# First group norm's scale behind the projection instead of ahead of it, with the opening's work in another order

## The reference, cut to what matters

```python
def reference(x, w_in, w_qk, w_outa, rel_bias, w_qkv, w_outb):
    x = x + A(gn(x), w_in, w_qk, w_outa, rel_bias)   # x is (4, 16, 16, 256), float32
    return x + B(gn(x), w_qkv, w_outb)

def gn(v):          # 32 groups of 8 channels; the statistics run over all 256 tokens and the 8 channels
    return (v - mean) / sqrt(var + 1e-5)

def A(x, ...):      # 8 heads of 16 rows, attention along the 256 channels
    xr = einsum('bcft,hc->bhft', x, w_in)   # x as (batch, 16 rows c, 16 columns f, 256 channels t)
    v = xr.transpose(...);  q, k = split(einsum('bct,dc->bdt', xr, w_qk))
    out = softmax((q @ k.T + bias[k_pos - q_pos]) / 4) @ v
    return einsum('bhft,ch->bcft', out, w_outa)

def B(x, ...):      # 16 heads of 16, tokens in chunks, each chunk sees itself and the one before
    ...
```

## Time and profile before

| | us |
|---|---|
| median of 3 runs | 181.91 |
| the profiled execution | 181.56 |
| its span in the trace | 179.8 |
| TensorE busy | 160.8 |
| VectorE busy | 140.9 |
| ScalarE busy | 103.3 |
| GpSimd busy | 84.1 |

### The profile page before, as it was taken

One profiled execution on the slowest core, in us unless ns is written; L12 is line 12 of the kernel. 1 busy time (PEld: TensorE's weight loads), 2 busy tenths in 40 slices (PEclk: granted clock), 3 DMA queues, 4 the chain that ended last, 5 costly groups with the idle time before them and its releaser, 6 DMA issues.

```text
span 179.8 us, 3978 instructions
## 1 busy us (share of the span) xinstructions
PE 160.8 (89%) x1434; PEld 123.0 (68%) x1434; DVE 140.9 (78%) x356; ACT 103.3 (57%) x225; POOL 84.1 (47%) x106
## 2 busy tenths in 40 slices
PE   0789679899989997999799999999999999999973
PEld 0289569778867786789668657777667876666551
DVE  1494878988794889687999899888989779888130
ACT  3103698578666764868575774757555684344420
POOL 0915439525624372512396286624484359455000
PEclk9999999999999999999999999999999999999999
DMA  4549300000000000000000000000000000100101
GB/s 116 195 137 344 106 0 5 0 0 4 2 0 0 5 0 2 4 0 0 0 0 4 0 0 7 0 4 0 0 33 29 4 0 29 33 2 25 37 10 52
DMA packets 4979, 5.34 MB, mean 30 GB/s; under 512 B 440, under 2 KB 4920, under 8 KB 4960
## 3 DMA queue, kind: packets, MB, share of 16 engines
q1 hardware_dynamic: 4496, 4.80, 8.2%
q10 hardware_dynamic: 464, 0.28, 0.7%
HBM read 4.02 MB, written 1.06 MB: 28 GB/s over the span
## 4 chain that ended last, share of the span: by engine, by line
PE 69%; DVE 17%; issue 5%; ACT 5%; DMA 2%; POOL 1%; DVEq 0%; POOLq 0%
PE bank L567 14%; PE bank L510 6%; PE bank L543 5%; PE bank L623 5%; PE bank L614 4%; PE bank L660 4%; PE bank L529 4%; PE bank L564 4%; PE bank L555 4%; DVE bank L882 4%; DVE bank L904 3%; PE bank L519 3%; ACT QM L1080 2%; PE bank L551 2%; PE bank L656 2%
## 5 line engine op out<-in xcount | busy, mean ns | idle before, releaser
L1101 ACT ACTIVATE PT<-bank 128x512 f32<-128x512 f32 x64 | 38.3, 601 | 42.7 <-PE bank L567 22.6
L343 POOL TENSOR_TENSOR Qk<-Qn,con 128x512 f32<-128x512 f32 x32 | 37.1, 1164 | 27.3 <-PE bank L567 26.9
L882 DVE CUSTOM_DVE_ANT_0 bank<-bank,Tk 128x256 f32<-128x256 f32 x64 | 25.8, 446 | 9.9 <-PE bank L529 9.9
L567 PE MATMUL bank<-Qk,Kf 128*128 128x512 f32 x64 | 32.6, 591 | 0.0
L894 DVE TENSOR_TENSOR D<-con,NM 128x512 fp32r<-128x512 f32 x32 | 28.9, 903 | 2.0 <-PE bank L567 1.9
L319 POOL TENSOR_TENSOR D<-con,NM 128x256 fp32r<-128x256 f32 x32 | 19.6, 620 | 20.0 <-PE bank L555 16.6
L886 DVE TENSOR_REDUCE NM<-bank 128x4 f32<-128x512 f32 x32 | 21.9, 683 | 1.9 <-PE bank L543 1.8
L904 DVE TENSOR_TENSOR bank<-bank,Tk 128x512 f32<-128x512 f32 x32 | 23.2, 725 | 0.0
L529 PE MATMUL bank<-KH,QM 128*128 128x256 f32 x64 | 15.1, 319 | 4.6 <-ACT QM L1080 4.6
L543 PE MATMUL bank<-Km,Qs 128*128 128x512 f32 x32 | 16.6, 520 | 0.0
L555 PE MATMUL bank<-QM,KL 128*128 128x256 f32 x64 | 16.5, 280 | 0.0
(11 more groups left out here) (136 smaller groups left out, 325.6 us busy)
## 6 DMA issues: line engine op xcount, KB each, us to landing
Tk<-bias_rows SPq DMA_DIRECT2D x4, 384.0 KB, 4.7
X<-x SPq DMA_DIRECT2D x4, 256.0 KB, 4.7
y<-Y SPq DMA_DIRECT2D x8, 128.0 KB, 1.7
Kf<-w_qkv SPq DMA_DIRECT2D x1, 768.0 KB, 7.8
Kf<-w_outb SPq DMA_DIRECT2D x1, 256.0 KB, 7.9
con<-consts ACTq DMA_DIRECT2D x1, 145.5 KB, 2.8
PT<-w_qk ACTq DMA_DIRECT2D x1, 128.0 KB, 4.4
PT<-buckets SPq DMA_DIRECT2D x1, 64.0 KB, 3.1
```

The lines of the kernel that those rows point to most:

```text
L343: nc.gpsimd.tensor_tensor(Qk[:, idx % QRING, :].rearrange("p (a v q) -> p v a q", a=4, v=2), Qn[:, b % 2, g, c * CHUNK:(c + 1) * CHUNK].un ...
L567: return nc.tensor.matmul(z[:], Kf[:, b % 3, g, w:w + 2 * CHUNK], Qk[:, (b * BLK + u) % QRING, :], start=False, stop=True, skip_group_chec ...
L882: last = V.tensor_tensor_reduce(half, half, Tk[:, u, nt * P:nt * P + CH], 1.0, LOWEST, ALU.add, ALU.max, NM[:, i % 2, 2 * u + nt:2 * u + n ...
L1101: A.activation(PT[:, u, :], bank[Z_BANK + u % 2][:], ACT.Exp, scale=SCALE).then_inc(p_ready, 1)
```

## The change

- The tile `Xn` is gone. TensorE projects the centred x (L449 reads `Xc`, which is the tile X1), waits for the centring alone, and VectorE multiplies the result by the scale into a new tile `XF` (`scaled_xr`, with the reversed order), one instruction of 128 x 256 for each of the four units. `XRh` and `XRl` are made from `XF`.
- The values are `XF` transposed: two transposes in place of four two-pass matmuls for each unit.
- The sums `Part` run over both token tiles in VectorE, so that `moments` is one matmul (two passes) and not two.
- For groups 1 and 2 the root is taken on GpSimd: VectorE adds eps (`vpe`), GpSimd raises 32 or 64 columns to the power -0.5 (`deviation`). Group 0 keeps Sqrt and reciprocal. The table load for Exp moves ahead of step 0.
- ScalarE makes the rounded weights of queries and keys and the copy `diag`.
- The fills of the value tiles `VB` on GpSimd move from the opening into steps 5 and 6.
- The transfers and the opening's work stand in another order.

```diff
-        Xn = sb("Xn", [P, BATCH, TT, CH])
+        Sq = sb("Sq", [P, BATCH, TT, CH])
         X1 = sb("X1", [P, BATCH, TT, CH])
-        Xc, Sq = X1, Xn
-        Part = sb("Part", [P, 2, BATCH, TT, GRP])
+        Xc = X1
+        Part = sb("Part", [P, 2, BATCH, GRP])
         Mu = sb("Mu", [P, BATCH, GRP])
-        Sd = sb("Sd", [P, BATCH, GRP])
+        Sd = sb("Sd", [P, GRP])
+        vpe = sb("vpe", [P, BATCH, GRP])
...
+        XF = sb("XF", [P, CH])
...
-            sp.dma_start(rb[:], rel_bias).then_inc(rb_in, 16)
-            sp.dma_start(hot, buckets).then_inc(hot_in, 16)
+            sp.dma_start(con[:], consts).then_inc(con_in, 16)
             for b in range(1, BATCH):
                 sp.dma_start(X[:, b], x[b].rearrange("(t p) c -> p t c", p=P)).then_inc(x_in[b], 16)
...
-            for n in range(2):
+
+            def value_fills(n):
...
-            pool.wait_ge(fills, 8)
...
-            def scale(g, b):
-                pool.wait_ge(rs_ready, g + 1)
-                nc.gpsimd.tensor_tensor(grouped(Xn, b)[:, :, ::-1, ::-1], grouped(Xc, b), spread(Rs, b), op=ALU.mult).then_inc(xn_pool, 1)
+            def deviation(g):
+
+                b0, b1 = GROUPS[g]
+                pool.wait_ge(fills, 2)
+                pool.wait_ge(vpe_ready, g)
+                nc.gpsimd.tensor_tensor(Rs[:, b0:b1].rearrange("p b g -> p (b g)"), vpe[:, b0:b1].rearrange("p b g -> p (b g)"),
+                                        mhalf[:, 0:1].to_broadcast([P, (b1 - b0) * GRP]), op=ALU.pow).then_inc(rs_pool, 1)
...
-            scale(1, 1)
+            deviation(1)
             for t in range(STEPS):
                 ahead = t - LAG + AHEAD
                 if 0 <= ahead < BATCH * BLK:
                     diagonal(ahead // BLK, ahead % BLK)
                 if BATCH * BLK <= ahead < UNITS * BLK:
                     head_queries(ahead // BLK, ahead % BLK)
-                if t in (3, 4):
-                    scale(2, t - 1)
+                if t == 3:
+                    deviation(2)
+                if t in (5, 6):
+                    value_fills(t - 5)
...
-                for t in range(TT):
-                    last = nc.tensor.matmul(bank[SUM_BANK[g]][:, col:col + (b1 - b0) * GRP], avg[:],
-                                            Part[:, which, b0:b1, t, :], start=(t == 0), stop=(t == TT - 1))
+                last = nc.tensor.matmul(bank[SUM_BANK[g]][:, col:col + (b1 - b0) * GRP], avg[:],
+                                        Part[:, which, b0:b1, :], start=True, stop=True)
...
-                        pe.wait_ge(xn_dve, 1)
-                        pe.wait_ge(small_ready, 2)
+                        pe.wait_ge(cent_ready, 1)
+                        pe.wait_ge(small_ready, 1)
                     else:
-                        pe.wait_ge(xn_pool, i)
+                        pe.wait_ge(cent_pool, i)
                     wait_bank_f(i)
                     for t in range(TT):
-                        last = nc.tensor.matmul(f[:, 0:CH], WinK[:, t, :], Xn[:, i, t, :], start=(t == 0), stop=(t == TT - 1))
+                        last = nc.tensor.matmul(f[:, 0:CH], WinK[:, t, :], Xc[:, i, t, :], start=(t == 0), stop=(t == TT - 1))
...
-                            last = nc.tensor.matmul(f[:, m * P:(m + 1) * P], Xn[:, i, t, m * P:(m + 1) * P], WinK[:, t, :],
-                                                    start=(t == 0), stop=(t == TT - 1))
+                        last = nc.tensor.transpose(f[:, m * P:(m + 1) * P], XF[:, m * P:(m + 1) * P], ident)
...
             moments(0, 0, part_ready, mean_done)
+            small_weights(0)
+            moments(1, 0, part_ready, mean_done)
+            query_key_weights()
             bias_rows()
-            query_key_weights()
             moments(0, 1, part2_ready, var_done)
-            small_weights()
-            moments(1, 0, part_ready, mean_done)
             project_a(0, 0)
+            small_weights(1)
...
-                if t == 1:
+                if t == 2:
                     moments(2, 1, part2_ready, var_done)
...
-                V.tensor_reduce(Part[:, which, b0:b1].rearrange("p b t g -> p (b t g)"),
-                                src[:, b0:b1].rearrange("p b t (g c) -> p (b t g) c", c=GC), AX.X, ALU.add).then_inc(done, 1)
+                for b in range(b0, b1):
+                    last = V.tensor_reduce(Part[:, which, b], src[:, b].rearrange("p t (g c) -> p g t c", c=GC), AX.XY, ALU.add)
+                last.then_inc(done, 1)
...
-                if step == 3:
-                    dve.wait_ge(sd_ready, g + 1)
-                    V.reciprocal(Rs[:, b0:b1], Sd[:, b0:b1]).then_inc(rs_ready, 1)
-                    if g == 0:
-                        dve.wait_ge(rs_ready, 1)
-                        V.tensor_tensor(grouped(Xn, 0)[:, :, ::-1, ::-1], grouped(Xc, 0), spread(Rs, 0), op=ALU.mult).then_inc(xn_dve, 1)
-
-            def small_weights():
+                if step == 3 and g == 0:
+                    dve.wait_ge(sd_ready, 1)
+                    V.reciprocal(Rs[:, 0], Sd[:]).then_inc(rs_ready, 1)
+                if step == 3 and g > 0:
+                    dve.wait_ge(var_done, g + 1)
+                    V.tensor_scalar(vpe[:, b0:b1].rearrange("p b g -> p (b g)"), m[:, 256:256 + (b1 - b0) * GRP],
+                                    EPS, None, ALU.add).then_inc(vpe_ready, 1)
...
+                dve.wait_ge(wqk_high, 2)
                 for k, (high, low) in enumerate(((WQh, WQl), (WKh, WKl))):
                     src = bank[S_BANK][:, 0:2 * P].rearrange("p (h k d) -> p h k d", k=2, d=HD)[:, :, k, :]
                     src = src.unsqueeze(2).to_broadcast([P, HA, 2, HD])
                     high, low = (w[:].rearrange("p t (h r d) -> p (t h) r d", r=2, d=HD) for w in (high, low))
-                    V.tensor_copy(high, src).then_inc(wqk_ready, 1)
-                    dve.wait_ge(wqk_ready, 2 * k + 1)
                     V.tensor_tensor(low, src, high.bitcast(F32), op=ALU.subtract).then_inc(wqk_ready, 1)
...
+            def scaled_xr(i):
+
+                dve.wait_ge(xr_done, i + 1)
+                if i == 0:
+                    dve.wait_ge(rs_ready, 1)
+                else:
+                    dve.wait_ge(rs_pool, min(i, 2))
+                    dve.wait_ge(v_done, i)
+                V.tensor_tensor(XF[:].rearrange("p (g c) -> p g c", c=GC)[:, ::-1, ::-1],
+                                bank[F_BANK][:, 0:CH].rearrange("p (g c) -> p g c", c=GC),
+                                Rs[:, i].unsqueeze(2).to_broadcast([P, GRP, GC]), op=ALU.mult).then_inc(xs_ready, 1)
 
             def low_xr(i):
 
                 dve.wait_ge(xr_ready, i + 1)
                 if i:
                     dve.wait_ge(k_done, i)
-                V.tensor_tensor(XRl[:], bank[F_BANK][:, 0:CH], XRh[:].bitcast(F32), op=ALU.subtract).then_inc(xrl_ready, 1)
+                V.tensor_tensor(XRl[:], XF[:], XRh[:].bitcast(F32), op=ALU.subtract).then_inc(xrl_ready, 1)
...
             norm_x(0, 0)
+            norm_x(1, 0)
             norm_x(0, 1)
-            dve.wait_ge(diag_done, 1)
-            V.tensor_copy(diag, bank[Z_BANK + 1][0:HA, :]).then_inc(diag_ready, 1)
+            small_weights(0)
+            norm_x(1, 1)
             norm_x(0, 2)
-            norm_x(1, 0)
             query_key_weights()
             norm_x(0, 3)
-            small_weights()
-            norm_x(1, 1)
             norm_x(2, 0)
+            scaled_xr(0)
+            norm_x(2, 1)
+            low_xr(0)
+            norm_x(1, 2)
+            small_weights(1)
             V.tensor_scalar(minus[:], con[:, C_ID:C_ID + P], 0.0, -1.0, ALU.mult, ALU.add).then_inc(rounded, 1)
-            low_xr(0)
-            norm_x(2, 1)
-            norm_x(1, 2)
             queries_keys(0, 0)
             queries_keys(0, 1)
             norm_x(1, 3)
...
-                    norm_x(2, 2)
                     value_rows(0)
                 if t == 1:
+                    norm_x(2, 2)
+                if t == 2:
                     norm_x(2, 3)
...
+                for i in due(t, XR_A, IN_A[1:]):
+                    scaled_xr(i)
...
-            act.dma_start(con[:], consts).then_inc(con_in, 16)
             act.dma_start(win[:], w_in).then_inc(win_in, 16)
+            act.dma_start(rb[:], rel_bias).then_inc(rb_in, 16)
+            act.dma_start(hot, buckets).then_inc(hot_in, 16)
+            act.dma_start(wqk, w_qk.rearrange("(a p) c -> p a c", p=P)).then_inc(wqk_in, 16)
             act.dma_start(wouta[:], w_outa).then_inc(wouta_in, 16)
-            act.dma_start(wqk, w_qk.rearrange("(a p) c -> p a c", p=P)).then_inc(wqk_in, 16)
...
+            def deviation():
+                act.wait_ge(var_done, 1)
+                A.activation(Sd[:], bank[SUM_BANK[0]][:, 256:256 + GRP], ACT.Sqrt, bias=eps[:]).then_inc(sd_ready, 1)
+
+            def high_weights():
+                act.wait_ge(wqk_done, 1)
+                for k, high in enumerate((WQh, WKh)):
```

(20 more changed lines are left out.)

59 lines of the change are left out of this document (31 added, 28 removed).

## The result

| | before | changed kernel |
|---|---|---|
| median | 181.91 us | 192.35 us (191.26 to 193.26) |
| ratio to before | | 1.0546, 95% interval [1.0489, 1.0604] |
| profiled execution, its span | 181.56 us | 193.08 us, span 191.3 us |
| mean granted clock of the span | | 0.95 |

Some executions run in a second, slower state, whatever the kernel; the medians and ratios of this document leave them out, and of the traces shown that of e10 is from such an execution.

The account below looks back on a forecast made before the run. TensorE was taken to bind, busy 89% of the span, with VectorE nearly full in part A. Gains of 2.3 (opening) and 0.7 (part A) from 181.56 gave 178.55, plus 0.35 for the median: 178.9 us, range 177.2 to 182.2.

Parts of the forecast that it names:

- The roots on GpSimd: Powers for groups 1 and 2: 22 ns a column, 1.4 and 2.1 us, charged at nothing.
- the slower rival: Roots above 62 ns a column use up the gain; 185.6 us at 100 ns; VectorE and TensorE idle; chance 0.16.
- The rooms: Time each GpSimd root may take before VectorE or TensorE waits: 1.8 us for the first, 2.1 for the second.
- the lower end: Root's price from below, growing like a multiplication: 1.9 ns a column, 0.8 us for 32 or 64 columns.
- The opening: Work up to first scores and first bias addition: 1.9 and 2.4 us earlier; 2.3 us gain taken.
- Part A: After the opening: shorter values gain 0.9 us, XF on VectorE costs 0.2, net gain 0.7.
- The subtraction from two tiles in SBUF: XRl in part A, possible contention with GpSimd: charged at nothing, at worst 0.4 us for each of three units.
- Part B: Later part, TensorE busy 75.4 of 76.0 us: nothing in it shortens, earlier arrival comes out as earlier end.
- the transfers behind the later bias table: Bias strips and part B's weights move about 2.5 us later, still in time: cost nothing.

Follow-up runs that it names:

- e10: e9 without its 18 matmuls whose result nobody reads; 182.88 us, ratio 1.0035 to the kernel before.
- e1: Changed kernel with roots of groups 1 and 2 by Sqrt on ScalarE and reciprocal on VectorE, Exp table load behind the second; 182.91 us, ratio 1.0020.
- e5: e1 plus 20 matmuls whose result nobody reads, where TensorE idles; 179.50 us, ratio 0.9852 to the kernel before.
- e9: Changed kernel with variances laid on 32 partitions, so GpSimd's powers have 1 and 2 columns, plus 18 matmuls nobody reads; 180.36 us, ratio 0.9902.

## Why the prediction was wrong

- **The step that failed is "The roots on GpSimd", by the size of one term.** It took 22 ns a column, which it called the geometric middle of 1.9 and 280 (that is 23, and changes nothing); the runs show 158. So the powers took 5.42 and 10.53 us and not 1.4 and 2.1, and the waits charged at nothing came to 4.0 us on VectorE and 5.7 on TensorE. The mechanism was right: what exceeds its room is lost, VectorE behind the first and TensorE behind the second, and the slower rival named these places, with 185.6 at 100 ns.
- **The rooms were not right, and their sum came close by luck.** With 1.8 and 2.1 and the measured lengths 12.0 us are lost, and the prediction's own sum gives 178.9 + 12.0 = 190.9, near the 192.35 measured. The changed kernel's rooms were 1.5 and 4.8, though, and 9.7 us were lost; 9.4 lie between e1 and it. TensorE came to its shift at 34.0, not at 27.2 plus the 3.6 lost before, in part, by the durations of its matmuls, because it worked at the lower level on the way. The 4.0 us that e1 is above the forecast make up the rest of the 13.4.
- **What was chosen badly** is the value between the ends. The row of 2 columns, 0.71 us, bounded the price from above at 0.28, and the lower end was the slope of simple operations (the prediction calls both multiplications; the row of 512 columns is the subtraction that centres x). That subtraction takes 1.08 and a power of 128 x 2 already 0.71. Two hundred and fifty-six times the columns for one and a half times the time was the sign that a power is of another kind. Of the two ends the upper was nearer, by a factor of 1.8 against 83. By the row that was nearest in kind, the slower case deserved far more than 0.16.
- **Not in the prediction at all: the length of TensorE's stretches at the lower level.** It knew of the lower level in the opening and went back to the higher one for the rest, as in the trace of before. With the roots short and no filler, e1 and e10 are at 182.9, 4.0 above the forecast; with filler e5 meets it, 179.5 against 178.9. In the changed kernel itself filler gave 1.4, which is not clear of noise.
- **The opening: right.** First projection, XRh, the queries and the first scores came within 0.35 us of the forecast. With the clock kept, in e5, the first bias addition is 1.8 earlier than before (25.73 against 27.52), forecast 2.4. The missing 0.6 fits the table load, which e5 has behind its second Sqrt and the changed kernel has not: TensorE waits 0.70 us at 24.49 for the masked query behind it.
- **Part A: right in size.** From the first bias addition to the last of part A, e5 gains 0.5 (60.88 against 61.40 us), forecast 0.7: 1.13 from the values, and some 0.6 back, where 0.2 was charged for `XF` (worked out as a difference; no run isolates it). The subtraction from two tiles in SBUF, open at up to 0.4 a unit, takes 0.41 each of four times. In e5 GpSimd was idle beside three of the four, so this does not test what the two engines cost each other when both work.
- **Part B, and the transfers behind the later bias table:** no cost, as charged. The first maximum of the changed kernel waits for TensorE and not for its strip, and e5's lead at the last bias addition of part A, 2.3 us (86.61 against 88.92), is its lead at the end (179.25 against 181.56). TensorE's 75.6 busy us of 76.0 in e5 are the 75.4 of before.

## What to carry to other kernels

Where one small instance of an operation is all that a trace shows, and its length is far from what a cheap operation of that size would take, charge it wholly by size until a run shows a start-up cost; a middle between the ends is no evidence. An operation on GpSimd that costs by columns should get its data across partitions, as in e9. And a wait put on TensorE should be priced twice, its length and the slower matmuls that may follow; where the next wait is for another engine, part of the second price is covered by it.

## What the runs showed of the hardware

- A power on GpSimd: 0.38 us and 158 ns a column, whether on 16 or 128 partitions, beside other work or alone; a multiplication of 32 columns 0.24 us.
- Matmuls whose result nobody reads, 20 of them, made a kernel 3.4 us faster (e5 against e1), of which some 1.2 us is not shown to be theirs. The 18 in e9 made 2.5 against e10.
- The granted clock's record can read 1.00 while the matmuls have the lower level's durations (e10, 0.63 us for a shift at 26.9; the changed kernel, 1.91 us for unit 1's projection at 18.72, where others have 1.03).
